# Layer 3's edge pass of a four-layer graph kernel: its shares and its weighed messages placed in PSUM

## The chip, the cores and the metric

The kernel runs on one core of one Trainium2 chip. The metric is the time of one execution in microseconds of the device; before the change it is 6999.95 us, the median of three runs (6999.25 to 7001.5).

The engines are named as in the profile: PE (TensorE), DVE (VectorE, "the vector engine"), ACT (ScalarE), POOL (GpSimd) and SP. Every engine works through its own queue of instructions in order, and waits on semaphores. A core has two memories that matter here: SBUF, and the smaller PSUM.

## The reference

Four graph layers follow one another, each with a residual and a layer norm. All use the same 100,000 edges, sorted by their target `dst`, over 6250 nodes of 128 features. The change touches the fourth layer, L3:

```python
h = x @ W
s_src, s_dst = h @ a_src, h @ a_dst
e = leaky_relu(s_src[src] + s_dst[dst], 0.2)      # one score per edge
m = segment_max(e, dst)
ex = exp(e - m[dst])
denom = segment_sum(ex, dst)
alpha = ex / denom[dst]
out = segment_sum(h[src] * alpha[:, None], dst) + bias
```

So a softmax over the edges that arrive at each node weighs the rows `h[src]`, which are then summed by target (self-loops are added to the edge list).

## The kernel before, in words

**Tiling.** The sorted edges are laid out as 128 partitions by `NC` = 784 columns: a partition holds 784 consecutive edges. Column j is one edge in each of the 128 partitions. Layers 0, 1 and 2 each make one pass over the edges with `sum_strands` (their tiles are named l0z, l1z and l2z); layer 3 makes its own with `sum_messages` (l3z), since its softmax is computed on the way: `Online3` carries along the columns the highest score so far, the sum of shares and the weighed sum of rows, and rescales the old sum by a factor each time the highest score moves.

**One batch of layer 3's pass.** `BATCHES` cuts the 784 columns into 48 batches of 16 and a last two of 8, 50 in all.

- POOL issues one indirect DMA for each column (line 777): it reads the column's 128 indices and starts a gather of 128 rows of 130 numbers from `table` in HBM into `rows`. `rows` is a ring of six batches; from the seventh on POOL first waits until the message product of the batch five before is done (`hold(pool, weighed, ...)`).
- The vector engine, once a batch has landed, computes the scores and the running maximum in seven small instructions on 128x16 (lines 824 to 830) and leaves two exponents per edge in `d`: plane 1 for the edge's share, plane 0 for the factor on the old sum.
- ACT takes the exponential of both planes in one instruction (line 838) into `xx`.
- The vector engine multiplies the 16 rows by their shares into `msg` in one instruction over 128x2048 (line 832), adds up the shares with a scan (line 833), and then makes 16 steps of line 753, one for each column: new sum = old sum x factor + message, into `acc`. Each step waits for the one before.
- SP stores `acc` to `prefix` in HBM, one store for each batch (line 785).

**Where the operands lie.** In layer 3's pass `rows`, `msg`, `acc`, `d` and `xx` are all in SBUF. In the passes of layers 0 to 2 the tiles `share`, `factors`, `keep` and `kept` are in PSUM (`s.ps` instead of `s.sb`), so that each of their large vector instructions has one tensor from SBUF and one from PSUM.

**What sets the order.** Nothing is planned at run time: each engine's program is written out in the order of the loops over `BATCHES`. After the pass comes `tail3` (l3y), whose first POOL instruction and first vector instructions wait until the pass's block has ended on every engine.

Of the kernel before, what the change touches and what calls it, by code (L numbers as in the profile page):

```python
# [5 lines left out]
P = 128  # L6
D = 128
# [29 lines left out]
ALU = mybir.AluOpType  # L37
ACT = mybir.ActivationFunctionType
# [44 lines left out]
def hold(eng, sem, value):  # L83

    eng.wait_ge(sem, value)
    eng.nop(nofuse=True)


class Chain:
# [32 lines left out]
    def __call__(self, ins, alone=False):  # L122
        self.add(ins)
        self.until(0, alone)
# [7 lines left out]
def bc_last(ap, n):  # L132

    return ap.unsqueeze(2).to_broadcast([ap.shape[0], ap.shape[1], n])
# [548 lines left out]
WIDTH, RING, ACCS = 16, 6, 2  # L683
# [23 lines left out]


def sum_messages(nc, name, g, order, table, prefix, width, weigh, aside):


    with Space(nc, name) as s:
        rows = s.sb("rows", [P, RING, WIDTH, width])
        msg = s.sb("msg", [P, WIDTH, D])
        wide = weigh.wide
        acc = s.sb("acc", [P, ACCS, WIDTH, wide])
        idx = s.sb("idx", [P, NC], I32)
        aside.psum(s)
        ys, us, es, weighed, summed = s.sem("ys"), s.sem("us"), s.sem("es"), s.sem("weighed"), s.sem("summed")
        indexed = s.sem("indexed")  # L720
        got = [s.sem(f"got{r}") for r in range(RING)]
        stored = [s.sem(f"sto{r}") for r in range(ACCS)]
        w = weigh(nc, s, us, es, weighed, order, rows, msg, acc)

        def landed(k):
            return 16 * sum(hi - lo for lo, hi in BATCHES[k % RING:k + 1:RING])

        def sum_before(k, u):
            if u:
                return acc[:, k % ACCS, u - 1]  # L730
            return acc[:, (k - 1) % ACCS, BATCHES[k - 1][1] - BATCHES[k - 1][0] - 1] if k else acc[:, ACCS - 1, WIDTH - 1]

        with s.block() as block:
            @block.vector
            def _(eng):
                v = nc.vector
                chain = Chain(eng, ys)
                aside.indices(v, chain, g, idx).then_inc(indexed, 1)
                chain(v.memset(acc[:, ACCS - 1], 0.0))
                w.start(chain)  # L740
                for k, (lo, hi) in enumerate(BATCHES):
                    c = k % ACCS
                    aside.on_vector(eng, chain, k)
                    eng.wait_ge(got[k % RING], landed(k))
                    if k >= ACCS:
                        eng.wait_ge(stored[c], (k // ACCS) * 16)
                    if lo:
                        eng.wait_ge(summed, lo)
                    w.weigh(eng, chain, k, lo, hi, sum_before(k, 0))
                    for u in range(hi - lo):  # L750
                        if lo + u:
                            eng.wait_ge(summed, lo + u)
                        v.scalar_tensor_tensor(acc[:, c, u, 0:D], sum_before(k, u)[:, 0:D], w.factor(k, lo, u), msg[:, u],  # L753
                                               ALU.mult, ALU.add).then_inc(summed, 1)
                eng.wait_ge(summed, NC)
                v.tensor_copy(g.tail[:, 0], sum_before(len(BATCHES), 0)[:, 0:D])
                w.end(sum_before(len(BATCHES), 0))

            @block.tensor
            def _(pe):  # L760
                aside.on_tensor(pe)

            @block.scalar
            def _(act):
                for k, (lo, hi) in enumerate(BATCHES):
                    aside.on_scalar(act, k)
                    w.on_scalar(act, k, hi - lo)

            @block.gpsimd
            def _(pool):  # L770
                pool.wait_ge(indexed, 1)
                for k, (lo, hi) in enumerate(BATCHES):
                    aside.on_pool(pool, k)
                    if k >= RING:
                        hold(pool, weighed, k - RING + 1)
                    for u in range(hi - lo):
                        nc.gpsimd.indirect_dma_start(out=rows[:, k % RING, u, :], out_offset=None, in_=table,  # L777
                                                     in_offset=bass.IndirectOffsetOnAxis(ap=idx[:, lo + u:lo + u + 1], axis=0)).then_inc(got[k % RING], 16)

            @block.sync  # L780
            def _(sp):
                out = prefix[0:EP].rearrange("(p j) f -> p (j f)", j=NC)
                for k, (lo, hi) in enumerate(BATCHES):
                    sp.wait_ge(summed, hi)
                    sp.dma_start(out[:, lo * wide:hi * wide], acc[:, k % ACCS, 0:hi - lo].rearrange("p u f -> p (u f)")).then_inc(stored[k % ACCS], 16)
                for r in range(ACCS):
                    sp.wait_ge(stored[r], 16 * len(range(r, len(BATCHES), ACCS)))


class Online3:  # L790
# [11 lines left out]
    def __call__(self, nc, s, us, es, weighed, order, rows, msg, acc):  # L802
        self.nc, self.us, self.es, self.acc = nc, us, es, acc
        self.rows, self.msg, self.v, self.order, self.weighed = rows, msg, nc.vector, order, weighed
        self.gap = s.sb("gap", [P, NC])
        self.most = s.sb("most", [P, NC + 1])
        self.e, self.old = s.sb("e", [P, WIDTH]), s.sb("old", [P, WIDTH])
        self.d = s.sb("d", [P, 2, 2, WIDTH])
        self.x = s.sb("xx", [P, 2, 2, WIDTH])
        return self  # L810

    def start(self, chain):
# [2 lines left out]
        chain(v.tensor_scalar(self.gap[:], self.order.keep[:], BIG, -BIG, ALU.mult, ALU.add))  # L815

    def factor(self, k, lo, u):
        return self.x[:, k % 2, 0, u:u + 1]

    def weigh(self, eng, chain, k, lo, hi, before):  # L820
        n, h = hi - lo, k % 2
        v, e, old, d, x = self.v, self.e[:, 0:n], self.old[:, 0:n], self.d[:, h, :, 0:n], self.x[:, h, :, 0:n]
        rows, out, gap, most = self.rows[:, k % RING, 0:n], self.acc[:, k % ACCS, 0:n], self.gap[:, lo:hi], self.most[:, 1 + lo:1 + hi]
        chain(v.tensor_tensor(e, rows[:, :, D], self.sd[:, lo:hi], ALU.add))  # L824
        chain(v.scalar_tensor_tensor(e, e, 0.2, e, ALU.mult, ALU.max))
        chain(v.tensor_tensor_scan(most, gap, e, self.most[:, lo:lo + 1], ALU.add, ALU.max))
        chain.add(v.tensor_tensor(d[:, 1], e, most, ALU.subtract))
        chain(v.tensor_tensor(old, gap, self.most[:, lo:hi], ALU.add))
        v.tensor_tensor(d[:, 0], old, most, ALU.subtract).then_inc(self.us, 1)
        chain.add(v.tensor_copy(out[:, :, D], most))  # L830
        eng.wait_ge(self.es, k + 1)
        v.tensor_tensor(self.msg[:, 0:n], rows[:, :, 0:D], bc_last(x[:, 1], D), ALU.mult).then_inc(self.weighed, 1)
        chain.add(v.tensor_tensor_scan(out[:, :, D + 1], x[:, 0], x[:, 1], before[:, D + 1:D + 2], ALU.mult, ALU.add))
        eng.wait_ge(self.weighed, k + 1)

    def on_scalar(self, eng, k, n):
        eng.wait_ge(self.us, k + 1)
        self.nc.scalar.activation(self.x[:, k % 2, :, 0:n], self.d[:, k % 2, :, 0:n], ACT.Exp).then_inc(self.es, 1)


STRANDS = 4
# [16 lines left out]


def sum_strands(nc, name, g, order, table, prefix, width, weigh, aside):  # L860


# [79 lines left out]
class Weighed:  # L942
# [12 lines left out]
    def weigh(self, eng, chain, k, lo, hi):  # L955
        n = STRANDS * (hi - lo)
        if k == 0:
            chain(self.v.tensor_copy(self.factors[:], by_step(self.weight)))
        rows, msg = by_strand(self.rows[:, k % RING, 0:n, 0:D]), by_strand(self.msg[:, 0:n])
        factor, half = self.factors[:, lo:hi].rearrange("p j c -> p c j"), STRANDS // 2  # L960
        chain.add(self.v.tensor_tensor(msg[:, 0:half], rows[:, 0:half], bc_last3(factor[:, 0:half], D), ALU.mult))  # L961
        self.v.tensor_tensor(msg[:, half:], rows[:, half:], bc_last3(factor[:, half:], D), ALU.mult).then_inc(self.weighed, 1)
        chain.until()
        eng.wait_ge(self.weighed, k + 1)
# [1618 lines left out]
```

## Time and profile before

| | |
|---|---|
| median of three runs | 6999.95 us |
| the profiled execution | 6994.2 us, of which its span 6992.3 us |
| POOL busy | 4840.2 us (69%) in 4959 instructions |
| DVE busy | 3985.8 us (57%) in 6763 instructions |
| ACT, PE busy | 718.2 us (10%), 1018.9 us (15%) |
| DMA | 33% to 34% of the 16 engines' time inside layer 3's pass |

A busy share is an average over all stages. Layer 3's pass is the stretch from about 5819 to 6868 us of the span, and it is read by itself below. In a row of a group of instructions the columns are: line, engine, operation, output and inputs, shapes and count, then after the bar busy us and mean ns of one, then the engine's idle time just before these instructions and what ended it. "issue" as a releaser means that the engine waited for nothing that the profile shows.

### The profile page before, as it was taken

What the parts mean: (1) busy time and instruction counts of PE and PEld (TensorE: products, weight loads), DVE (VectorE), ACT (ScalarE), POOL (GpSimd) and SP (SyncE); (2) the same over time, 40 slices, a digit from 0 to 9 for tenths busy, and PEclk for the clock granted to TensorE, in tenths of its full rate; (3) what the DMA queues carried; (4) which work ended last, traced back from release to release, by engine and by line L of the source; (5) the groups of instructions that cost most, each with busy time, mean ns of one, the idle gap of its engine ahead of it and who ended that gap; (6) DMA issues with size and microseconds to landing.
All of it is one profiled execution on the core that took longest, in us unless ns stands there. A gap on an engine that the chain in (4) does not pass through costs nothing. (4 is left out here: it accounts for less than half of the span.)

```text
span 6992.3 us, 25324 instructions
## 1 busy us (share of the span) xinstructions
PE 1018.9 (15%) x4502; PEld 685.1 (10%) x4502; DVE 3985.8 (57%) x6763; ACT 718.2 (10%) x1445; POOL 4840.2 (69%) x4959
## 2 busy tenths in 40 slices
PE   7520127000000000000068840000000010000000
PEld 5520126000000000000033310000000010000000
DVE  8999998434444443344347677785344363444446
ACT  1013333000000000000034420000000030000002
POOL 0037777677777677777767777777777777777775
PEclk9999669555555555555579975555555555555555
DMA  3055000234444333333339964324333322333332
GB/s 57 1 194 192 2 11 2 59 95 112 106 110 112 98 114 102 106 107 104 100 127 341 350 244 122 118 76 112 107 107 105 102 76 77 99 99 99 105 99 70
DMA packets 594551, 772.09 MB, mean 110 GB/s; under 512 B 122203, under 2 KB 483521, under 8 KB 574809
## 3 DMA queue, kind: packets, MB, share of 16 engines
q1 hardware_dynamic: 416916, 375.57, 16.9%
q0 software_dynamic: 159264, 283.89, 16.3%
q10 hardware_dynamic: 18210, 111.02, 4.1%
q14 instruction: 125, 1.02, 0.0%
q8 instruction: 36, 0.59, 0.0%
HBM read 357.94 MB, written 412.16 MB: 110 GB/s over the span
## 5 line engine op out<-in xcount | busy, mean ns | idle before, releaser
L777 POOL DMA_INDIRECT l3z_rows<-table,l3z_idx x784 | 803.0, 1024 | 249.3 <-issue 238.5
L928 POOL DMA_INDIRECT l2z_rows<-proj,l2z_idx x784 | 766.1, 977 | 246.5 <-issue 238.6
L928 POOL DMA_INDIRECT l0z_rows<-table,l0z_idx x784 | 742.8, 947 | 249.0 <-issue 235.8
L928 POOL DMA_INDIRECT l1z_rows<-table,l1z_idx x784 | 740.0, 944 | 248.0 <-issue 238.5
L2469 POOL DMA_INDIRECT l2s_krow<-table_k,l2s_idx x784 | 741.9, 946 | 238.9 <-issue 234.6
L1917 POOL DMA_INDIRECT first_sj<-scores,first_atdst x544 | 542.7, 998 | 182.1 <-issue 182.1
L2436 PE MATMUL l2s_bank<-l2o_wr,l2o_xT 128*128 128x512 f32 x800 | 377.4, 626 | 93.1 <-ACT l2s_proj L2448 78.2
L961 DVE TENSOR_TENSOR l1z_msg<-l1z_rows,l1z_factors 128x1024 f32<-128x1024 f32 (+1 forms) x50 | 60.0, 1200 | 553.9 <-DMA l1z_rows<-table,l1z_idx 553.9
L961 DVE TENSOR_TENSOR l2z_msg<-l2z_rows,l2z_factors 128x1024 f32<-128x1024 f32 (+1 forms) x50 | 60.0, 1200 | 513.0 <-DMA l2z_rows<-proj,l2z_idx 512.6
L824 DVE TENSOR_TENSOR l3z_e<-l3z_rows,l3h_sd 128x16 f32<-128x16 f32 (+1 forms) x50 | 9.6, 192 | 551.9 <-DMA l3z_rows<-table,l3z_idx 551.9
L595 POOL IOTA sd_nidi<- 128x50 int32 x1 | 0.2, 171 | 430.2 <-POOLq L60 430.2
L984 DVE TENSOR_TENSOR l0z_a<-l0z_rows,mid_sjd 128x64 f32<-128x64 f32 (+1 forms) x50 | 13.6, 272 | 495.1 <-DMA l0z_rows<-table,l0z_idx 495.1
L753 DVE SCALAR_TENSOR_TENSOR l3z_acc<-l3z_acc,l3z_xx,l3z_msg 128x128 f32<-128x128 f32 x784 | 277.2, 354 | 26.1
L2420 DVE TENSOR_TENSOR l2s_prod<-l2s_krow,l2s_qrow 128x1024 f32<-128x1024 f32 x98 | 119.6, 1221 | 254.9 <-DMA l2s_krow<-table_k,l2s_idx 254.9
L2448 ACT COPY l2s_proj<-l2s_bank 128x1024 f32<-128x1024 f32 x200 | 197.9, 1013 | 273.9 <-DMA proj<-l2s_proj 161.6
L244 DVE TENSOR_TENSOR prep_key<-prep_key 128x512 f32<-128x512 f32 x292 | 202.4, 693 | 5.6
L245 DVE TENSOR_TENSOR prep_key<-prep_key 128x512 f32<-128x512 f32 x292 | 202.4, 693 | 0.0
L2436 PEld LDWEIGHTS l2s_bank<-l2o_wr,l2o_xT 128*128 128x128 f32 x800 | 154.9, 199 | 315.2 <-issue 169.8
L2411 DVE TENSOR_TENSOR l2s_qrow<-l2s_qrow,l2s_zrow 128x656 f32<-128x656 f32 x196 | 166.5, 849 | 6.7
L2410 DVE TENSOR_TENSOR l2s_qrow<-l2s_qrow,g_dokeep 128x656 f32<-128x656 f32 x195 | 165.7, 849 | 6.9 <-DVE l_base L2423 0.3
L1665 PE MATMUL l3y_cpr<-g_ident,l3h_ends 128*128 128x128 f32 x4 | 1.2, 453 | 1090.7 <-PEq L60 1090.7
L1136 PE MATMUL l0y_cps<-g_ident,g_tail 128*128 128x128 f32 x4 | 1.1, 427 | 1060.5 <-PEq L60 1060.5
(578 smaller groups left out, 5191.4 us busy)
## 6 DMA issues: line engine op xcount, KB each, us to landing
proj<-l2s_proj ACTq DMA_DIRECT2D x100, 1024.0 KB
spread_q<-prep_zero SPq DMA_DIRECT2D x98, 656.0 KB
l2s_zrow<-spread_q SPq DMA_DIRECT2D x98, 656.0 KB
prefix<-l0z_acc SPq DMA_DIRECT2D x196, 256.0 KB
prefix<-l1z_acc SPq DMA_DIRECT2D x196, 256.0 KB
prefix<-l2z_acc SPq DMA_DIRECT2D x196, 256.0 KB
prefix<-l3z_acc SPq DMA_DIRECT2D x48, 1040.0 KB
l0z_rows<-table,l0z_idx POOLq DMA_INDIRECT x784
```

Source lines behind the costliest of these rows:

```text
L244: v.tensor_tensor(new_lo, hi, lo, ALU.min).then_inc(self.ranked, 1)
L245: v.tensor_tensor(new_hi, hi, lo, ALU.max).then_inc(self.ranked, 1)
L753: v.scalar_tensor_tensor(acc[:, c, u, 0:D], sum_before(k, u)[:, 0:D], w.factor(k, lo, u), msg[:, u], ALU.mult, ALU.add).then_inc(summed, 1)
L777: nc.gpsimd.indirect_dma_start(out=rows[:, k % RING, u, :], out_offset=None, in_=table, in_offset=bass.IndirectOffsetOnAxis(ap=idx[:, lo + ...
L928: nc.gpsimd.indirect_dma_start(out=rows[:, k % RING, c * (hi - lo) + u, :], out_offset=None, in_=table, in_offset=bass.IndirectOffsetOnAxi ...
L961: chain.add(self.v.tensor_tensor(msg[:, 0:half], rows[:, 0:half], bc_last3(factor[:, 0:half], D), ALU.mult))
L1917: nc.gpsimd.indirect_dma_start(out=sj[:, j, :], out_offset=None, in_=g.scores0, in_offset=bass.IndirectOffsetOnAxis(ap=at_dst[:, j:j + 1], ...
L2410: chain(v.tensor_tensor(q[:, :, u], last, bc_last(by_step(order.keep[:])[:, lo + u], QROW), ALU.mult))
L2411: v.tensor_tensor(q[:, :, u], q[:, :, u], z[:, :, u], ALU.add).then_inc(stepped, 1)
L2436: mm = nc.tensor.matmul(bank[m % 2][:, b], xT[:, i, :], wr[:, c:c + wide], start=True, stop=True)
L2448: nc.scalar.copy(proj[:, c], bank[m % 2][:].rearrange("p b f -> p (b f)")).then_inc(copied, 1)
L2469: nc.gpsimd.indirect_dma_start(out=krow[:, k % KRING, c * (hi - lo) + u, :], out_offset=None, in_=g.table_k, in_offset=bass.IndirectOffset ...
```

## The change

Two tiles of layer 3's pass move from SBUF to PSUM: `msg`, the weighed messages of a batch, and a new tile `share`, which holds the shares that were plane 1 of `xx`. The single activation over both planes becomes two: the first writes `share`, the second writes `xx`, which now holds the factors only. Both count up the semaphore `es`, so that the vector engine waits for 2(k+1) instead of k+1. The message product (line 832) and the scan of the shares (line 833) take `share`; line 753 takes `msg` from PSUM, and its text stays as it is.

```diff
-        msg = s.sb("msg", [P, WIDTH, D])
+        msg = s.ps("msg", [P, WIDTH, D])
...
-        self.x = s.sb("xx", [P, 2, 2, WIDTH])
+        self.x, self.share = s.sb("xx", [P, 2, WIDTH]), s.ps("share", [P, 2, WIDTH])
...
     def factor(self, k, lo, u):
-        return self.x[:, k % 2, 0, u:u + 1]
+        return self.x[:, k % 2, u:u + 1]
...
-        eng.wait_ge(self.es, k + 1)
-        v.tensor_tensor(self.msg[:, 0:n], rows[:, :, 0:D], bc_last(x[:, 1], D), ALU.mult).then_inc(self.weighed, 1)
-        chain.add(v.tensor_tensor_scan(out[:, :, D + 1], x[:, 0], x[:, 1], before[:, D + 1:D + 2], ALU.mult, ALU.add))
+        eng.wait_ge(self.es, 2 * (k + 1))
+        v.tensor_tensor(self.msg[:, 0:n], rows[:, :, 0:D], bc_last(share, D), ALU.mult).then_inc(self.weighed, 1)
+        chain.add(v.tensor_tensor_scan(out[:, :, D + 1], x, share, before[:, D + 1:D + 2], ALU.mult, ALU.add))
...
     def on_scalar(self, eng, k, n):
         eng.wait_ge(self.us, k + 1)
-        self.nc.scalar.activation(self.x[:, k % 2, :, 0:n], self.d[:, k % 2, :, 0:n], ACT.Exp).then_inc(self.es, 1)
+        self.nc.scalar.activation(self.share[:, k % 2, 0:n], self.d[:, k % 2, 1, 0:n], ACT.Exp).then_inc(self.es, 1)
+        self.nc.scalar.activation(self.x[:, k % 2, 0:n], self.d[:, k % 2, 0, 0:n], ACT.Exp).then_inc(self.es, 1)
```

No instruction moves past another. On the vector engine, in the first full batch of layer 3's pass, the difference in the written order is in two names (lines with - are before, with + after):

```order
 L829 TENSOR_TENSOR l3z_d<-l3z_old,l3z_most 128x16
 L830 COPY l3z_acc<-l3z_most 128x16
-L832 TENSOR_TENSOR l3z_msg<-l3z_rows,l3z_xx 128x2048
-L833 SCALAR_TENSOR_TENSOR l3z_acc<-l3z_xx,l3z_acc 128x16
+L832 TENSOR_TENSOR l3z_msg<-l3z_rows,l3z_share 128x2048
+L833 SCALAR_TENSOR_TENSOR l3z_acc<-l3z_xx,l3z_acc,l3z_share 128x16
 L753 SCALAR_TENSOR_TENSOR l3z_acc<-l3z_acc,l3z_xx,l3z_msg 128x128 x16
 L824 TENSOR_TENSOR l3z_e<-l3z_rows,l3h_sd 128x16
```

The sequence and the count stay; `share` stands where `xx` stood (line 833 is the scan). On ACT the 50 activations of the pass become 100, two in a row for each batch; POOL's and SP's queues are unchanged but for line numbers (lines below 838 move down by one).

## Rows read from the trace of the kernel before

**Rows 1.** Groups of instructions, layer 3's pass (5819 to 6872 us); columns as above.
```profile
L777 POOL DMA_INDIRECT l3z_rows<-table,l3z_idx x784 | 803.0, 1024 | 249.3 <-issue 238.5 <-DVE l3z_idx L691 10.7
L753 DVE SCALAR_TENSOR_TENSOR l3z_acc<-l3z_acc,l3z_xx,l3z_msg 128x128 f32<-128x128 f32 x784 | 277.2, 354 | 26.1
L832 DVE TENSOR_TENSOR l3z_msg<-l3z_rows,l3z_xx 128x2048 f32<-128x2048 f32 (+1 forms) x50 | 112.5, 2250 | 10.0 <-ACT l3z_xx L838 9.7
```
**Rows 2.** Waits in the same stretch: us in total, times, longest us.
```profile
DVE l3z_e L824 <- DMA l3z_rows<-table,l3z_idx: 551.9, 50, 18.7
POOL l3z_rows L777 <- issue: 238.5, 783, 0.3
```
**Rows 3.** Layer 3's gathers by tile: duration ns min/median/max, first and last start us.
```profile
L777 POOL DMA_INDIRECT l3z_rows<-table,l3z_idx x784: 940/945/2271, 5819.1 to 6859.7; - x196
```
**Rows 4.** Timeline of one batch of 16: start us, us, engine, line, [idle before <-releaser].
```profile
6117.04 0.23 DVE L824 TENSOR_TENSOR l3z_e<-l3z_rows,l3h_sd 128x16 f32<-128x16 f32 x1 [11.17 <-DMA l3z_rows<-table,l3z_idx]
...
6118.31 0.95 POOL L777 DMA_INDIRECT l3z_rows<-table,l3z_idx  x1 [0.30 <-issue]
6118.57 2.29 DVE L832 TENSOR_TENSOR l3z_msg<-l3z_rows,l3z_xx 128x2048 f32<-128x2048 f32 x1 [0.20 <-ACT l3z_xx L838]
6119.56 2.11 POOL L777 DMA_INDIRECT l3z_rows<-table,l3z_idx  x1 [0.30 <-issue]
...
6120.94 6.18 DVE L753 SCALAR_TENSOR_TENSOR l3z_acc<-l3z_acc,l3z_xx,l3z_msg 128x128 f32<-128x128 f32 x16
6121.98 0.94 POOL L777 DMA_INDIRECT l3z_rows<-table,l3z_idx  x1 [0.30 <-issue]
...
6125.73 1.05 POOL L777 DMA_INDIRECT l3z_rows<-table,l3z_idx  x1 [0.30 <-issue]
...
6138.38 0.18 DVE L824 TENSOR_TENSOR l3z_e<-l3z_rows,l3h_sd 128x16 f32<-128x16 f32 x1 [11.26 <-DMA l3z_rows<-table,l3z_idx]
```
**Rows 5.** Layer 1's pass by tile: duration ns min/median/max, first and last start us.
```profile
L928 POOL DMA_INDIRECT l1z_rows<-table,l1z_idx x784: 940/945/962, 2491.2 to 3470.0; - x196
L961 DVE TENSOR_TENSOR l1z_msg<-l1z_rows,l1z_factors x50: 689/1222/1223, 2514.0 to 3472.4; 128x1024 f32<-128x1024 f32 x48, 128x512 f32<-128x512 f32 x2
L962 DVE TENSOR_TENSOR l1z_msg<-l1z_rows,l1z_factors x50: 679/1214/1217, 2515.2 to 3473.0; 128x1024 f32<-128x1024 f32 x48, 128x512 f32<-128x512 f32 x2
L902 DVE TENSOR_TENSOR l1z_kept<-l1z_acc,l1z_keep x196: 695/695/697, 2516.5 to 3475.3; 128x512 f32<-128x512 f32 x196
L903 DVE TENSOR_TENSOR l1z_acc<-l1z_kept,l1z_msg x196: 690/691/693, 2517.2 to 3476.0; 128x512 f32<-128x512 f32 x196
```
**Rows 6.** Layer 0's gathers by tile, same columns.
```profile
L928 POOL DMA_INDIRECT l0z_rows<-table,l0z_idx x784: 940/945/1246, 1413.6 to 2394.0; - x196
```
**Rows 7.** Timeline of the end of layer 3's pass and of `tail3`'s first instructions.
```profile
6854.62 1.01 POOL L777 DMA_INDIRECT l3z_rows<-table,l3z_idx  x1 [0.30 <-issue]
...
6859.68 0.94 POOL L777 DMA_INDIRECT l3z_rows<-table,l3z_idx  x1 [0.30 <-issue]
6862.19 0.17 DVE L824 TENSOR_TENSOR l3z_e<-l3z_rows,l3h_sd 128x8 f32<-128x8 f32 x1 [4.28 <-DMA l3z_rows<-table,l3z_idx]
...
6863.35 0.22 ACT L838 ACTIVATE l3z_xx<-l3z_d 128x16 f32<-128x16 f32 x1 [9.81 <-DVE l3z_d L829]
6863.60 1.23 DVE L832 TENSOR_TENSOR l3z_msg<-l3z_rows,l3z_xx 128x1024 f32<-128x1024 f32 x1 [0.20 <-ACT l3z_xx L838]
...
6864.89 3.05 DVE L753 SCALAR_TENSOR_TENSOR l3z_acc<-l3z_acc,l3z_xx,l3z_msg 128x128 f32<-128x128 f32 x8
...
6872.18 0.94 POOL L1089 DMA_INDIRECT l3y_leadrow<-prefix,g_doleadi  x1 [11.55 <-POOLq L60]
```
**Rows 8.** Timeline, `tail3`: a vector step with one operand in PSUM, and two ACT instructions in a row.
```profile
6879.88 0.35 DVE L1713 SCALAR_TENSOR_TENSOR l3y_leadrow<-l3y_cps,l3y_cf,l3y_leadrow 128x128 f32<-128x128 f32 x1
...
6902.40 0.39 ACT L1176 ACTIVATE l3y_nsq<-l3y_agg,l3y_nm 128x128 f32<-128x128 f32 x1
6902.69 0.19 ACT L1176 ACTIVATION_READ_ACCUMULATOR l3y_nsq<-l3y_agg,l3y_nm 128x1 f32 x1
```

More of the change, by code:

```diff
@@ L817, in factor @@
     def factor(self, k, lo, u):
-        return self.x[:, k % 2, 0, u:u + 1]
+        return self.x[:, k % 2, u:u + 1]
     def weigh(self, eng, chain, k, lo, hi, before):
         n, h = hi - lo, k % 2
-        v, e, old, d, x = self.v, self.e[:, 0:n], self.old[:, 0:n], self.d[:, h, :, 0:n], self.x[:, h, :, 0:n]
+        v, e, old, d, x, share = self.v, self.e[:, 0:n], self.old[:, 0:n], self.d[:, h, :, 0:n], self.x[:, h, 0:n], self.share[:, h, 0:n]
         rows, out, gap, most = self.rows[:, k % RING, 0:n], self.acc[:, k % ACCS, 0:n], self.gap[:, lo:hi], self.most[:, 1 + lo:1 + hi]
```

## The prediction

> **What bounds the kernel now.** I read the page's costliest groups first: the six costliest are POOL's gathers. Then the groups and waits of the changed stretch alone. There POOL issues 784 gathers, busy 803.0 us, and its idle time before them is 238.5 us of "issue", a steady 0.30 us between two gathers, and no wait but the one at the start [rows 1, 2]. The vector engine waits 551.9 us for gathered rows, at every one of the 50 batches [rows 2]. So POOL's issuing sets the length of the pass: from the first gather to the last 6859.7 - 5819.1 = 1040.6 us [rows 3]. The ring never holds POOL up, and the vector engine has about 11 us free in each batch [rows 4].
>
> Next I asked why a gather takes 803.0/784 = 1024 ns here. By tile its median is 945 ns and its longest 2271 ns [rows 3]. The timeline of a batch shows which ones are long: the gather that starts while the message product (line 832, 2.29 us) runs takes 2.11 us, and one of those among the 16 sums takes 1.05 us; the others take 0.94 or 0.95 us [rows 4]. The long gather starts at 6119.56, the product ends at 6118.57 + 2.29 = 6120.86, the gather at 6121.67: it ends 0.81 us after the product, as if it had stopped 0.13 us into its work until the product was done. The gather before it, at 6118.31, had passed that point when the product started, and is not delayed.
>
> The passes of the other layers are the comparison. Layer 1's gathers have the same median but a longest of 962 ns, though its vector engine runs products of 1.22 us and sums of 0.69 us beside them [rows 5]. What differs is where the operands lie: there each large vector instruction takes one tensor from SBUF and one from PSUM, in layer 3's pass both come from SBUF. Layer 0's pass, with a few 128x64 instructions on two SBUF tensors per batch, has a longest of 1246 ns [rows 6]. The trace therefore says that a vector instruction with two tensors in SBUF stops a gather's issue, and that one with a PSUM tensor does not.
>
> **The change, part by part.**
>
> *Message product and its share (line 832).* One gather in each of 48 full batches now takes 2.11 us or a little more (up to 2.27) where 0.945 was due: 2.11 - 0.945 = 1.17, some 1.19 with the longer ones, x 48 = 57 us. The two batches of 8 give almost nothing: the first delays a gather to 1.01 us, and during the last no gather is left [rows 7]. After the change the product reads `rows` from SBUF and `share` from PSUM, the operands of layer 1's line 961, beside which no gather passes 962 ns. I take the whole 57 us. Its own duration stays: 1222 ns for half the size in layer 1 against 1.23 us here [rows 5, 7]; a PSUM output costs nothing to see either (line 902 writes PSUM in 695 ns, line 903 SBUF in 691).
>
> *The 16 sums (line 753).* One gather per batch at 1.05 us (6125.73, [rows 4]) instead of 0.945: 0.105 x 48 = 5.0 us. The old sum stays in SBUF, the message comes from PSUM, and the factor is one number per partition in SBUF. No row before has just this mix beside a gather, so bounds: from 0 (if the factor counts as a second SBUF tensor) to 5.0. Line 903, one tensor from either memory, delays nothing, and the factor is a single number; I take 5.0. The check on both terms: all excess is 803.0 - 784 x 0.945 = 62.1 us, and 57 + 5 = 62.
>
> *The small instructions (lines 824 to 829)* keep two SBUF tensors. They delay nothing now, and they stay at the same place against the gathers, as both follow from the landing of the batch; 0. Layer 0's longer ones give the upper bound: its pass took 2394.0 - 1413.6 = 980.4 us against 3470.0 - 2491.2 = 978.8 in layer 1 [rows 5, 6], so at most 1.6 us.
>
> *What is late next.* With no stall the pass goes at POOL's own pace, 0.945 + 0.305 us per gather, 20.0 us per batch instead of 21.3. The vector engine needs 10.1 us of that (6117.04 to 6127.12), so it waits for rows as before, and the ring's hold stays met: a batch's product comes some 1.5 us after its landing, four batches ahead of the gather that needs its place. Layer 1's pass has run at this pace, gather for gather, over the same indices and with rows of 128 numbers instead of 130, so I expect no queue behind POOL to become the limit. By layer 1's pass the first-to-last time is 978.8, a gain of 1040.6 - 978.8 = 61.8; by layer 0's 60.2; by the excess 62.1. I take 62.
>
> *The second activation and its wait.* The vector engine now waits for two ACT instructions. Behind that wait stand the product, the scan, the sums and then SP's store, for which nobody waits until the end. 49 times it lies in the vector engine's spare time. Once, in the last batch, it lies on the path: the chain there goes from the last landing at 6862.19 over ACT at 6863.35, the product and eight sums to 6867.94, and POOL's next instruction (6872.18) waits for the end of the pass [rows 7]. Two ACT instructions in a row overlap by 0.1 us (0.39 long, the next starts 0.29 later, [rows 8]), so a second one of 0.22 adds 0.1 to 0.22: 0.2.
>
> *The sums at the end.* Eight dependent steps read PSUM. A step with a PSUM operand and a factor takes 0.35 us in line 1713 [rows 8], as line 753 does from SBUF (354 ns, [rows 1]). So 0 to 0.1 for the ten instructions; I take 0.1. The Trainium skill weighs against the change here: the page "Perfetto Trace Analysis", section "Optimizing Scalar/DVE Operations", puts the vector engine's access overhead at about 60 ns on SBUF and 125 ns on PSUM. By it ten instructions in the last batch would add an estimated 0.65 us, and the gain would be 61.2. This trace doesn't show that difference.
>
> Sum: -62 + 0.2 + 0.1 = -61.7 us. The profiled execution took 6994.2 us (6992.3 span and 1.9 around it), so 6932.5 in its terms. It lies 5.8 us below the median of the runs; the stall is the same in both, so I subtract from the median: 6999.95 - 61.7 = 6938.
>
> **The rivals.**
>
> A, *the sums go on delaying a gather*: a factor in SBUF beside an old sum in SBUF is enough. For it: line 753's mix stands beside no gather before the change. Against: the factor is one number per partition, read once. Gain 57 - 0.3; 6943.
>
> B, *the product goes on stopping its gather*: what stops it isn't the second SBUF tensor but that the engine reads long rows from SBUF, or writes much at once. For it: the product of 2048 per partition is the longest of its kind; layer 1's are 1024. Against: two of those stand back to back in layer 1 (1222 + 1214 ns), longer together, and still no gather passes 962 ns [rows 5]. Then only the sums' 5 us are won: 6995, within what a run can tell from no change. The Trainium skill has a sentence that would lead here too: in "SBUF — State Buffer", section "Who interferes with whom", a probe saw a tensor_copy stall such DMAs but a tensor_tensor not, since descriptors need only the write side. By that the stall would not be the product's at all, and moving its operand would win nothing. The trace disagrees: line 832 is a tensor_tensor, and the gather beside it takes 2.11 us.
>
> C, *the gathers' landing becomes the pace*, and half of the gain is lost behind it: 6969. For it: rows of 130 numbers, and a store of the sums in one large piece per batch, where layer 1 makes four. Against: the 16 DMA engines are busy a third of the time.
>
> D, slower: *the chain of sums becomes the bound.* Place: line 753 in the vector engine's queue, each step waiting for the one before. If a read of `msg` from PSUM drew the step out, the batch of 10.1 us would grow by 16 times that. It decides from 20.0 - 10.1 = 9.9 us, 0.62 per step, and is slower than before from (21.3 - 10.1)/16 = 0.70 on. At 0.8 a batch takes 22.9 us: 48 x 1.6 = 77 us more, 7077. Against: line 1713's 0.35 us.
>
> **How the numbers follow.** Forecast 6938: 84%. A 8%, B 4%, C 3%, D 1%. A measurement of this kernel tells about 0.2% (14 us) from no change. The forecast, A and C are faster by more: 0.95. B is the same: 0.04, D slower: 0.01. The range takes in the forecast and A. Low end: all of 63 us (if a gather costs 944 ns throughout), from the lowest run, 6999.25 - 63 = 6936, less 5.8 for how far a single execution has lain off the median: 6930. High end: A's 6943, the 1.6 of the small instructions, and the runs' spread of 2.25: 6947.
>
> **What would show it.** Right: layer 3's gathers have a longest below 1.1 us and a sum near 741 us; the pass's first-to-last time is about 979 us; line 832 stays near 2.3 us and line 753 near 0.354; the vector engine still waits for the gathers 50 times, in all about 60 us less. A would show a gather of about 1.05 us per batch among the sums; B one of 2.1 us beside line 832; C gathers at 945 ns with POOL waiting on a semaphore, or landings that come later; D vector instructions with no wait for gathers. The prediction is wrong if the gathers' median itself rises, or if the saved time comes back after the pass, in `tail3`, whose instructions are unchanged.

## The result, and the profile after

The changed kernel takes 6935.69 us, the median of four runs (6934.32 to 6936.35); the kernel before, with a fourth run beside it, 7000.46 us (6999.25 to 7001.5). The ratio is 0.9907, with a 95% interval from 0.989 to 0.9924. The forecast was 6938, in a range from 6930 to 6947.

The groups of instructions in layer 3's pass of the changed kernel (columns as in [rows 1]):

```profile
L777 POOL DMA_INDIRECT l3z_rows<-table,l3z_idx x784 | 740.7, 945 | 249.3 <-issue 238.6 <-DVE l3z_idx L691 10.7
L753 DVE SCALAR_TENSOR_TENSOR l3z_acc<-l3z_acc,l3z_xx,l3z_msg 128x128 f32<-128x128 f32 x784 | 271.7, 347 | 25.9
L832 DVE TENSOR_TENSOR l3z_msg<-l3z_rows,l3z_share 128x2048 f32<-128x2048 f32 (+1 forms) x50 | 112.7, 2253 | 14.2 <-ACT l3z_xx L839 14.2
```

POOL's 784 gathers take 740.7 us instead of 803.0 [rows 1], 62.3 us less, and the issue time between them is the same. The vector engine's long instructions kept their length within 2%. The waits (us in total, times, longest):

```profile
DVE l3z_e L824 <- DMA l3z_rows<-table,l3z_idx: 491.6, 49, 18.8
POOL l3z_rows L777 <- issue: 238.6, 783, 0.3
```

The vector engine still waits for rows in nearly every batch, 60.3 us less in all than in [rows 2]: the time it waited for is gone, not moved. By tile (duration ns min/median/max, first and last start us):

```profile
L777 POOL DMA_INDIRECT l3z_rows<-table,l3z_idx x784: 940/945/964, 5822.0 to 6800.4; - x196
```

The longest gather fell from 2271 ns [rows 3] to 964, and the pass from first to last gather from 1040.6 to 6800.4 - 5822.0 = 978.4 us. One batch on the timeline, to be laid beside [rows 4]:

```profile
6123.24 0.18 DVE L824 TENSOR_TENSOR l3z_e<-l3z_rows,l3h_sd 128x16 f32<-128x16 f32 x1 [10.08 <-DMA l3z_rows<-table,l3z_idx]
...
6124.46 0.19 ACT L838 ACTIVATE l3z_share<-l3z_d 128x16 f32<-128x16 f32 x1 [19.77 <-DVE l3z_d L829]
6124.58 0.20 ACT L839 ACTIVATE l3z_xx<-l3z_d 128x16 f32<-128x16 f32 x1
6124.81 2.30 DVE L832 TENSOR_TENSOR l3z_msg<-l3z_rows,l3z_share 128x2048 f32<-128x2048 f32 x1 [0.23 <-ACT l3z_xx L839]
6125.62 0.95 POOL L777 DMA_INDIRECT l3z_rows<-table,l3z_idx  x1 [0.30 <-issue]
6126.87 0.94 POOL L777 DMA_INDIRECT l3z_rows<-table,l3z_idx  x1 [0.30 <-issue]
...
6127.17 6.08 DVE L753 SCALAR_TENSOR_TENSOR l3z_acc<-l3z_acc,l3z_xx,l3z_msg 128x128 f32<-128x128 f32 x16
```

Two gathers start inside the product, at 6125.62 and 6126.87, and neither is delayed. The end of the pass answers to [rows 7]:

```profile
6800.38 0.94 POOL L777 DMA_INDIRECT l3z_rows<-table,l3z_idx  x1 [0.30 <-issue]
6803.03 0.17 DVE L824 TENSOR_TENSOR l3z_e<-l3z_rows,l3h_sd 128x8 f32<-128x8 f32 x1 [4.05 <-DMA l3z_rows<-table,l3z_idx]
...
6804.19 0.18 ACT L838 ACTIVATE l3z_share<-l3z_d 128x8 f32<-128x8 f32 x1 [9.53 <-DVE l3z_d L829]
6804.30 0.19 ACT L839 ACTIVATE l3z_xx<-l3z_d 128x8 f32<-128x8 f32 x1
6804.52 1.23 DVE L832 TENSOR_TENSOR l3z_msg<-l3z_rows,l3z_share 128x1024 f32<-128x1024 f32 x1 [0.29 <-ACT l3z_xx L839]
...
6805.80 3.02 DVE L753 SCALAR_TENSOR_TENSOR l3z_acc<-l3z_acc,l3z_xx,l3z_msg 128x128 f32<-128x128 f32 x8
...
6813.06 0.94 POOL L1090 DMA_INDIRECT l3y_leadrow<-prefix,g_doleadi  x1 [11.74 <-POOLq L60]
```

From the last gather to POOL's next instruction it is 6813.06 - 6800.38 = 12.68 us, before 6872.18 - 6859.68 = 12.50: the end costs 0.18 us more. So the pass with its end is 62.0 us shorter, by these two profiles. Most of the 0.18 is not the change's: the last rows landed 6803.03 - 6800.38 = 2.65 us after the last gather started, before 2.51 [rows 7]. From that landing to POOL's next instruction it is 10.03 us, before 9.99.

The kernel before took 7000 us on the chip of this comparison and 6993 on the chip of the experiments below. So each experiment is compared with the runs of before on its own chip, and, where less than 0.2% decides, by the length of the pass in its profile, which agreed to 1 us in two profiles of the changed kernel (978.4 and 977.5).

### The profile page after: what moved, and what is told of

It reads as the page before. It is cut to its first block and busy times, and to the rows that moved or that the text cites. A ratio compares the mean times of both kernels' runs of the same rounds, so it can differ in the third digit from the quotient of the medians.

```text
span 6933.4 us, 25374 instructions
## 1 busy us (share of the span) xinstructions
PE 1035.4 (15%) x4502; PEld 693.1 (10%) x4502; DVE 3979.1 (57%) x6763; ACT 723.8 (10%) x1495; POOL 4782.2 (69%) x4959
## 5 line engine op out<-in xcount | busy, mean ns | idle before, releaser
L777 POOL DMA_INDIRECT l3z_rows<-table,l3z_idx x784 | 740.7, 945 | 249.3 <-issue 238.6
L929 POOL DMA_INDIRECT l1z_rows<-table,l1z_idx x784 | 740.7, 945 | 248.1 <-issue 238.6
L2437 PE MATMUL l2s_bank<-l2o_wr,l2o_xT 128*128 128x512 f32 x800 | 393.6, 651 | 98.4 <-ACT l2s_proj L2449 82.2
```

What stands on the lines that cost most here:

```text
L929: nc.gpsimd.indirect_dma_start(out=rows[:, k % RING, c * (hi - lo) + u, :], out_offset=None, in_=table, in_offset=bass.IndirectOffsetOnAxi ...
L2437: mm = nc.tensor.matmul(bank[m % 2][:, b], xT[:, i, :], wr[:, c:c + wide], start=True, stop=True)
```

## The experiments

Two theories stood. The first: a vector instruction that takes two tensors from SBUF stops a gather's issue until it ends. The rival: the product's long run of writing to SBUF, or reading from it, makes the stop. Two runs take the two placements apart, a third has neither.

**The shares alone in PSUM.** `msg` goes back to SBUF:

```diff
-        msg = s.ps("msg", [P, WIDTH, D])
+        msg = s.sb("msg", [P, WIDTH, D])
```

> The shares alone in PSUM, the messages back in SBUF: the product has one tensor in SBUF, the sums have two. Theory (a vector instruction with two tensors in SBUF stops a gather until it ends): no gather of 2.1 us beside the product; the sums go on delaying some, each sum by at most about 0.13 us, so a longest gather of about 1.1 us and 0 to 30 us for the pass, most likely about 5: first-to-last about 984 us (978 after the change, 1040.6 before), time about 6941. Rival B (writing or reading long rows of SBUF stops the gather): 2.1 us stay, pass near 1036, time about 6995.

Measured: 6937.46 us against 6993.28 before, ratio 0.992 (0.9904 to 0.9937). Its gathers by group (columns as in [rows 1]), by tile, and a batch:

```profile
L777 POOL DMA_INDIRECT l3z_rows<-table,l3z_idx x784 | 745.7, 951 | 249.3 <-issue 238.6 <-DVE l3z_idx L691 10.7
```

```profile
L777 POOL DMA_INDIRECT l3z_rows<-table,l3z_idx x784: 940/944/1072, 5819.4 to 6802.7; - x196
```

```profile
6123.46 2.29 DVE L832 TENSOR_TENSOR l3z_msg<-l3z_rows,l3z_share 128x2048 f32<-128x2048 f32 x1 [0.29 <-ACT l3z_xx L839]
6124.36 0.94 POOL L777 DMA_INDIRECT l3z_rows<-table,l3z_idx  x1 [0.30 <-issue]
...
6130.61 1.05 POOL L777 DMA_INDIRECT l3z_rows<-table,l3z_idx  x1 [0.30 <-issue]
```

The pass takes 983.3 us. The product reads the same rows and writes SBUF as before, and no gather beside it is longer than the rest; only the place of its second operand differs. The gather of 1.05 us among the sums is still there: the sums still have two tensors in SBUF. The gathers are busy for 745.7 - 740.7 = 5.0 us more than in the profile of the result, and for 745.7 - 739.9 = 5.8 us more than in that of the change on this chip (its rows stand with the last run below).

**The messages alone in PSUM.**

```diff
-        self.x, self.share = s.sb("xx", [P, 2, WIDTH]), s.ps("share", [P, 2, WIDTH])
+        self.x, self.share = s.sb("xx", [P, 2, WIDTH]), s.sb("share", [P, 2, WIDTH])
```

> The messages alone in PSUM, the shares in SBUF (still by an activation of their own): the product reads two tensors from SBUF and writes PSUM, the sums have one in SBUF. Theory: one gather per batch still takes 2.1 us, those among the sums 0.945; pass about 1036 us, time about 6995. Rival B (the write into SBUF stops the gather): no long gather, pass about 979, time about 6936.

Measured: 6992.02 us against 6993.28, ratio 0.9999 (0.9989 to 1.0008).

```profile
L777 POOL DMA_INDIRECT l3z_rows<-table,l3z_idx x784: 940/944/2447, 5815.1 to 6855.5; - x196
```

```profile
6114.78 2.30 DVE L832 TENSOR_TENSOR l3z_msg<-l3z_rows,l3z_share 128x2048 f32<-128x2048 f32 x1 [0.30 <-ACT l3z_xx L839]
6115.65 2.24 POOL L777 DMA_INDIRECT l3z_rows<-table,l3z_idx  x1 [0.30 <-issue]
```

The long gather stays although the product writes PSUM, so it isn't the write. The gathers among the sums are all undelayed in this batch. But the pass takes 1040.4 us, not the 1036 expected: the long gather grew from 2.11 us [rows 4] to 2.24. The next run tells why.

**Two activations, both tiles in SBUF** (both edits above together):

> Two activations, both tiles in SBUF: the change without the placement. Theory: as before the change, pass about 1040.8 us with one gather of 2.1 and one of 1.05 us per batch, time 7000. Rival (the gain comes from splitting the activation, or from the new time of the product against the gathers): pass below 1030.

Measured: 6999.15 us against 6993.28, ratio 1.0008 (0.9998 to 1.0018), no difference that the runs can tell; the pass took 1046.2 us, 5.6 more than before, where 0.2 was expected.

```profile
L777 POOL DMA_INDIRECT l3z_rows<-table,l3z_idx x784: 940/944/2832, 5820.0 to 6866.2; - x196
```

```profile
6120.94 0.20 ACT L839 ACTIVATE l3z_xx<-l3z_d 128x16 f32<-128x16 f32 x1
6121.18 2.29 DVE L832 TENSOR_TENSOR l3z_msg<-l3z_rows,l3z_share 128x2048 f32<-128x2048 f32 x1 [0.30 <-ACT l3z_xx L839]
6122.03 2.25 POOL L777 DMA_INDIRECT l3z_rows<-table,l3z_idx  x1 [0.30 <-issue]
```

In all 48 full batches, before and here, the stopped gather ends 0.81 to 0.83 us after the product, so the stop ends with the product. The second activation lets the product start 0.1 us later (0.30 us of wait instead of 0.20, [rows 4]), the stopped gather ends that much later (2.25 us instead of 2.11), and that is paid in each batch. The passes of these three runs and of the change on the same chip make a table (first to last gather, us):

| | `msg` in SBUF | `msg` in PSUM |
|---|---|---|
| `share` in SBUF | 1046.2 | 1040.4 |
| `share` in PSUM | 983.3 | 977.5 |

The shares' place is worth 62.9 us and the messages' 5.8, in either order.

**The product cut in four, everything in SBUF.** If the stop lasts only while one instruction runs, smaller instructions must shorten it without any PSUM. The kernel before, with

```diff
-        v.tensor_tensor(self.msg[:, 0:n], rows[:, :, 0:D], bc_last(x[:, 1], D), ALU.mult).then_inc(self.weighed, 1)
+        q = n // 4
+        for c in range(4):
+            ins = v.tensor_tensor(self.msg[:, c * q:(c + 1) * q], rows[:, c * q:(c + 1) * q, 0:D], bc_last(x[:, 1, c * q:(c + 1) * q], D), ALU.mult)
...
+        ins.then_inc(self.weighed, 1)
```

> The kernel before, with the message product cut into 4 instructions of 4 columns, everything in SBUF. Theory (the stop lasts only until the instruction in progress ends, and then the gather goes on): no gather is delayed by more than about 0.6 us; as the gather's read comes about 1.1 us after the product's start, in the second piece, I expect 0.1 to 0.6 us per batch instead of 1.19: pass 988 to 1016 us, time 6945 to 6975. Rival (a gather stays stopped while the product as a whole lasts, or as long as two-SBUF instructions follow each other): 2.1 us stay, pass about 1040.

Measured: 6945.94 us against 6993.28, ratio 0.9933 (0.9916 to 0.9949); the pass 993.3 us.

```profile
L777 POOL DMA_INDIRECT l3z_rows<-table,l3z_idx x784: 940/944/1277, 5817.8 to 6811.1; - x196
```

```profile
6124.70 2.50 DVE L834 TENSOR_TENSOR l3z_msg<-l3z_rows,l3z_xx 128x512 f32<-128x512 f32 x4 [0.20 <-ACT l3z_xx L843]
6125.61 1.20 POOL L777 DMA_INDIRECT l3z_rows<-table,l3z_idx  x1 [0.30 <-issue]
```

The gather is held for 0.26 us and then gets in between two pieces, though the next piece follows at once: the stop is that of one instruction, not of the product as a whole. This alone is worth 47 us.

**The other way round in layer 1.** The changed kernel, with layer 1's factors taken from PSUM to SBUF:

```diff
-        self.factors = s.ps("factors", [P, STRIDE, STRANDS])
+        self.factors = (s.sb if s.name == "l1z" else s.ps)("factors", [P, STRIDE, STRANDS])
```

> The kernel after the change, and in layer 1's pass the other way round: its factors go from PSUM to SBUF, so that its two products of 1.22 us per batch (lines 962 and 963) read two tensors from SBUF. Theory: the stop appears there. A gather starts with the first product, and its read comes 0.13 us later: stopped for about 1.1 us until the product ends, 48 times, 52 us; if it had to wait for the second product too, 2.2 us and 106 us. Layer 1's pass first-to-last 1030 us (to 1085), 978.8 before; time 52 us (to 106) above the change's. Rival (layer 3's rows of 130 numbers or its sums make the stop, not the placement): layer 1's pass stays at 979 us.

Measured: 6968.10 us (6965.91 to 6973.51) against 6929.97 for the change on the same chip, 38 us more. Layer 1's gathers, and one batch:

```profile
L929 POOL DMA_INDIRECT l1z_rows<-table,l1z_idx x784: 940/944/2002, 2491.6 to 3514.1; - x196
```

```profile
3393.66 0.94 POOL L929 DMA_INDIRECT l1z_rows<-table,l1z_idx  x1 [0.30 <-issue]
3393.69 1.22 DVE L962 TENSOR_TENSOR l1z_msg<-l1z_rows,l1z_factors 128x1024 f32<-128x1024 f32 x1 [12.75 <-DMA l1z_rows<-table,l1z_idx]
3394.83 1.22 DVE L963 TENSOR_TENSOR l1z_msg<-l1z_rows,l1z_factors 128x1024 f32<-128x1024 f32 x1
3394.90 1.96 POOL L929 DMA_INDIRECT l1z_rows<-table,l1z_idx  x1 [0.30 <-issue]
```

The stop appears in a pass that had none [rows 5]: 2.0 us instead of 0.945, and the pass grows from 978.7 to 1022.5 us. The size was off: 43.8 us, not 52. The expectation had the first product stop the gather that starts with it. In this batch that gather, which starts 0.03 us before the product, slips through, and the next one is held by the second product for 1.0 us. Over the pass one gather is held for about 1.0 us in 43 of the 48 full batches, which makes up the 43.8, and none in the other five. A gather that starts up to 0.02 us after a product still slips through, and one that starts 0.05 to 0.4 us after it is held, so such a count hangs on hundredths of a microsecond.

The profiled run is the slowest of its five, 43.1 us above the change's profiled run (6973.51 against 6930.45); the medians lie 38 apart. That more gathers slipped through in the other runs would explain this, but no trace shows it.

**The rule put to use in layer 2's attention.** Five instructions over 128x3136 beside layer 2's first gathers are cut into four each, in the changed kernel; the edit of one of the five:

```diff
-        chain(v.tensor_tensor(fwd[:], fwd[:], bwd[:], ALU.add))
+        for r in range(RULES):
+            chain.add(v.tensor_tensor(fwd[:, r], fwd[:, r], bwd[:, r], ALU.add))
+        chain.until()
```

> The kernel after the change, and in layer 2's attention, which runs beside the first gathers of layer 2's pass, five vector instructions over 128x3136 with two tensors in SBUF (3.42 us each, beside which gathers take 3.16 to 4.20 us) cut into four of 128x784 each. Nothing else changes. Theory (a stop lasts until the instruction in progress ends): no gather above about 2.4 us there, those beside the pieces near 1.4; the five long ones give up some 15 us, about 12 gathers pay 0.5 us each: a gain of about 9 us; layer 2's pass first-to-last about 995 us instead of 1005, time about 9 us below the change's. Rival (two-SBUF instructions that follow one another stop a gather as one): pass stays at 1005, time the same.

The change itself ran beside it, for the comparison:

> The change itself on this chip, to compare e5 and e6 with: about 60 us below the kernel before, layer 3's pass 978 us, layer 2's 1005.

Measured: 6923.46 us (6922.86 to 6924.70), the change 6929.97 (6929.32 to 6930.76), the kernel before 6993.19; ratios to before 0.9902 (0.9886 to 0.9917) and 0.991 (0.9896 to 0.9924). The runs of the two don't overlap: 6.5 us less, a version that beats both kernels. Layer 3's gathers of the change on this chip, as a group and by tile:

```profile
L777 POOL DMA_INDIRECT l3z_rows<-table,l3z_idx x784 | 739.9, 944 | 249.3 <-issue 238.6 <-DVE l3z_idx L691 10.7
L777 POOL DMA_INDIRECT l3z_rows<-table,l3z_idx x784: 940/944/961, 5818.5 to 6796.0; - x196
```

Layer 2's gathers, first of the change, then of the version in pieces:

```profile
L929 POOL DMA_INDIRECT l2z_rows<-proj,l2z_idx x784: 940/944/4163, 4643.0 to 5646.5; - x196
```

```profile
L929 POOL DMA_INDIRECT l2z_rows<-proj,l2z_idx x784: 940/944/2403, 4642.4 to 5639.3; - x196
```

The pass went from 1003.5 to 996.9 us, a gain of 6.6 where 9 was expected. No gather takes over 2.41 us any more. Those beside the pieces take 1.46 to 1.72 us, and there are more of them; two take 2.40 us, beside instructions that were left whole.

## Why the prediction was right

**What bounds the pass.** POOL's issuing, as read: the gathers lost 62.3 us of busy time and the pass 62.2 us, one for one. On the chip of the experiments both lost 63.1.

**The product: 57 us.** With the shares alone in PSUM the gathers were busy for 745.7 us, so the product's part was 803.0 - 745.7 = 57.3. The cause, two tensors in SBUF, is shown by taking it away (shares alone), by leaving it and moving the write (messages alone), and by bringing it to layer 1.

**The sums: 5.0 us.** Measured 5.0 to 5.8, the rest of the excess in that run (5.8 against the change on the same chip). Rival A is out: with the factor in SBUF beside the old sum, no gather after the change exceeds 964 ns.

**The small instructions: 0.** They are in the 740.7 us, 945 ns per gather; nothing is left to give them.

**Next in line.** POOL's own pace, 978.4 us against the 978.8 of layer 1 that the sum rested on. Rival C is out, and so is D: a step of line 753 takes 347 ns, and the vector engine waits for rows 49 times.

**The second activation: 0.2 us, once.** It was sized too high. From the last landing to the product's start it is 6804.52 - 6803.03 = 1.49 us, before 1.41 [rows 7]: 0.08 us more, below the 0.1 that the prediction had as the least. But the reason given, that 49 of the 50 lie in the vector engine's spare time, was incomplete. The spare time covers them only because nothing waits for the product's end any more. With a stopped gather waiting for it, as before the change, the same activation costs 5.6 us in the pass of the run with both tiles in SBUF. An instruction on an engine with time to spare was not free while another engine was held by what it delays.

**The sums at the end: 0.1 us more.** They got shorter by 0.03 us instead: they take 3.02 us instead of 3.05 [rows 7], 347 ns each instead of 354 [rows 1]. The Trainium skill's page "Perfetto Trace Analysis", section "Optimizing Scalar/DVE Operations", has PSUM as the slower access for the vector engine; for this instruction the trace shows it 7 ns faster.

**Rival B** falls by the same runs: with the shares alone in PSUM the product reads the same long rows and writes as much to SBUF, and no gather beside it is stopped. A row beside the attention shows it too, in the changed kernel:

```profile
4709.92 19.75 DVE L2327 RECIPROCAL l2b_fwd<-l2b_fwd 128x3136 f32<-128x3136 f32 x1
4711.01 0.94 POOL L929 DMA_INDIRECT l2z_rows<-proj,l2z_idx  x1 [0.30 <-issue]
4712.26 0.95 POOL L929 DMA_INDIRECT l2z_rows<-proj,l2z_idx  x1 [0.30 <-issue]
```

A reciprocal reads and writes SBUF for 19.75 us with one tensor as input, and gathers beside it take 0.94 and 0.95 us.

**The number.** The sum was 61.7 us off the median. The medians moved by 64.8 on the chip of the result and by 63.2 on that of the experiments, where the pass of the change, 63.1 us shorter than in the profile before, accounts for it. The 62.0 from the profile of the result is somewhat low: the passes of layers 0 to 2, which the change leaves alone, took 0.9, 0.7 and 1.6 us longer in that profile than in the one before, so these two executions did not run at quite the same pace. Some 2 to 3 us of the 64.8 remain unexplained. The 5.8 us by which the profile before lay under its median went into the low end of the range as the scatter of single executions. But the runs of before lie at most 3.3 us off their median on either chip, and the medians of the chips lie 7 us apart, so a difference between chips is the likelier source; that isn't shown.

## What to carry to other kernels

When GpSimd's issuing of gathers sets the pace, compare the longest gather with the median before anything else: the long ones name the vector instruction that stops them, by where it ends. Give a product or sum of two tensors at most one tensor from SBUF, which was enough for the two here, or cut it into short ones, which won 47 of the 62 us here and needs no PSUM. And an instruction that delays the end of such a stopping instruction costs that delay each time, 0.1 us in each batch here, even if its own engine is mostly idle.

## What was not expected of the hardware

A vector instruction with a single tensor can stop a gather too. In the version in pieces, a tensor_scalar on one SBUF tensor holds one until it ends:

```profile
4672.52 1.79 DVE L2304 TENSOR_SCALAR l2b_bwd<-l2b_bwd 128x3136 f32<-128x3136 f32 x1
4672.72 2.40 POOL L929 DMA_INDIRECT l2z_rows<-proj,l2z_idx  x1 [0.30 <-issue]
```

The gather ends at 4672.72 + 2.40 = 4675.12, 0.81 us after the tensor_scalar (4672.52 + 1.79 = 4674.31), as with the products. It goes through 3136 numbers in 1.79 us, 0.57 ns each, where the two-tensor products need 1.1 and the reciprocal, which stops nothing, 6.3. In the Trainium skill, page "SBUF — State Buffer", section "Who interferes with whom", tensor_scalar and copies that run in a faster mode with both ports are said to block GpSimd as well; this row agrees. The same section says that an instruction with two SBUF inputs contends with a GpSimd instruction that reads SBUF; all the runs above agree with that sentence, since each gather here takes its indices from the tile `idx` in SBUF. The section's remark that a tensor_tensor did not stall such DMAs, which the prediction put against the change, does not hold for these gathers.

In the changed kernel the same instruction, there on line 2301, stops a gather at another point:

```profile
4670.69 3.42 DVE L2300 TENSOR_TENSOR l2b_fwd<-l_qv,l_base 128x3136 f32<-128x3136 f32 x1
4671.89 4.16 POOL L929 DMA_INDIRECT l2z_rows<-proj,l2z_idx  x1 [0.31 <-issue]
4674.14 1.79 DVE L2301 TENSOR_SCALAR l2b_bwd<-l2b_bwd 128x3136 f32<-128x3136 f32 x1
```

This gather had been held by the two-tensor instruction of line 2300, which ended at 4674.11, and would have ended 0.81 us later, at 4674.92. It ends at 4671.89 + 4.16 = 4676.05, which is 0.12 us after the tensor_scalar (4674.14 + 1.79 = 4675.93). So the tensor_scalar holds a gather that the two-tensor instruction has let go; this was read in two profiles, and no run tests it.
